# Attention outputs kept transposed, scaled in memory by GpSimd, and unit loads by eight transfers

## What is computed

```python
x = x + attention(layernorm(x), ctx, ctx)       # x, ctx: 8 x 256 x 512
x = x + ffn(layernorm(x))

# attention: 32 heads of 16, 8 key/value groups (4 heads share one)
score = einsum('bhqd,bhkd->bhqk', qh, kh) / sqrt(16)
out = einsum('bhqk,bhkd->bhqd', softmax(score), vh)
return out.transpose(0, 2, 1, 3).reshape(N, S, 512) @ Wfc.T + bfc

# ffn: router over 8 experts (2 chosen, limited by groups), gated experts of
# width 352, plus a shared gated network of width 704
return routed + (silu(h @ sg.T) * (h @ su.T)) @ sd.T
```

## Time and profile before

| what | value |
|---|---|
| median of three runs | 791.12 us |
| the profiled execution's own time | 791.93 us |
| its span, first to last instruction | 790.1 us |
| busy: TensorE, VectorE, ScalarE, GpSimd | 760.1, 579.7, 429.3, 269.3 us |
| granted TensorE clock, mean | 0.994 |
| DMA, mean over the span | 218 GB/s |

### The profile page before, as it was taken

One profiled execution on the slowest core, in us unless ns is written; L12 is line 12 of the kernel. 1 busy time (PEld: TensorE's weight loads), 2 busy tenths in 40 slices (PEclk: granted clock), 3 DMA queues, 4 the chain that ended last, 5 costly groups with the idle time before them and its releaser, 6 DMA issues.

```text
span 790.1 us, 16078 instructions
## 1 busy us (share of the span) xinstructions
PE 760.1 (96%) x5151; PEld 407.0 (52%) x5152; DVE 579.7 (73%) x1194; ACT 429.3 (54%) x843; POOL 269.3 (34%) x224
## 2 busy tenths in 40 slices
PE   6998999999999989999999999999999999999897
PEld 4553533343433325656755556555555555555553
DVE  4777779999999976998789886555555555547666
ACT  3666579999999973566433553434344343322231
POOL 3263008999993301665300101111111111015331
PEclk9999989999999999999999999999999999999999
DMA  8898846556645798998598576876777777559985
GB/s 330 324 405 245 250 139 211 185 168 194 195 121 172 228 331 295 331 376 275 173 232 225 137 173 137 187 174 175 183 175 180 179 180 173 126 164 288 288 240 150
DMA packets 161782, 172.07 MB, mean 218 GB/s; under 512 B 103680, under 2 KB 117504, under 8 KB 161216
## 3 DMA queue, kind: packets, MB, share of 16 engines
q1 hardware_dynamic: 150012, 128.89, 56.5%
q0 software_dynamic: 11120, 41.43, 16.8%
q10 hardware_dynamic: 596, 1.07, 0.4%
HBM read 105.40 MB, written 42.73 MB: 187 GB/s over the span
## 4 chain that ended last, share of the span: by engine, by line
PE 77%; DVE 10%; DMA 7%; ACT 2%; issue 2%; SPq 1%; DVEq 0%; ACTq 0%
PE psum L1467 29%; PE psum L1479 15%; PE psum L1317 8%; PE psum L1303 6%; PE psum L1231 4%; PE psum L1403 4%; PE psum L1207 4%; PE psum L1334 2%; DMA sb_weights<-in_wdn 2%; DMA sb_weights<-attn_dram 2%; PE psum L1183 1%; DMA sb_hT<-sb_h 1%; DMA sb_weights<-x_dram 1%; DMA sb_weights<-in_ctxT 1%; DVE sb_rows L1902 1%
## 5 line engine op out<-in xcount | busy, mean ns | idle before, releaser
L1467 PE MATMUL psum<-sb_weights,sb_rows 128*128 (+1 forms) x1608 | 250.8, 313 | 0.5 <-DMA sb_rows<-xnT_dram 0.5
L1467 PEld LDWEIGHTS psum<-sb_weights,sb_rows 128*128 128x128 f16 x1608 | 157.2, 98 | 91.8 <-DMA sb_rows<-xnT_dram 1.0
L1027 ACT ACTIVATE sb_weights<-psum,sb_rows 128x512 f32<-128x512 f32 x256 | 158.3, 683 | 16.9 <-PE psum L1303 15.0
L1699 DVE TENSOR_REDUCE sb_rows<-psum 128x4 f32<-128x1024 f32 x128 | 149.9, 1213 | 5.5 <-PE psum L1231 5.5
L1479 PE MATMUL psum<-sb_weights,sb_hT 128*128 (+1 forms) x630 | 147.4, 379 | 2.2 <-DMA sb_hT<-sb_h 2.2
L894 POOL DMA_INDIRECT sb_rows<-xn_rows,sb_slot_tok x39 | 38.2, 980 | 218.1 <-DVE sb_rows L2288 147.9
L1479 PEld LDWEIGHTS psum<-sb_weights,sb_hT 128*128 128x128 f16 x630 | 61.4, 98 | 67.5 <-DMA sb_hT<-sb_h 3.1
L1303 PE MATMUL psum<-sb_weights 50*128 50x512 f16 x256 | 90.0, 391 | 3.0 <-ACT sb_weights L1027 2.6
L1096 ACT ACTIVATE psum<-psum 128x352 f32<-128x352 f32 x71 | 31.8, 448 | 111.8 <-DVE psum L1949 111.8
L1317 PE MATMUL psum<-sb_weights 128*32 128x256 f32 x1024 | 82.9, 396 | 0.0
L1231 PE MATMUL psum<-sb_weights 48*128 48x256 f16 x512 | 73.2, 275 | 0.5 <-DVE sb_rows L1699 0.4
(11 more groups left out here) (264 smaller groups left out, 1017.9 us busy)
## 6 DMA issues: line engine op xcount, KB each, us to landing
sb_weights<-in_wgu SPq DMA_DIRECT2D x20, 704.0 KB, 7.4
sb_weights<-in_wgu POOLq DMA_DIRECT2D x20, 704.0 KB, 5.6
sb_weights<-in_wdn SPq DMA_DIRECT2D x17, 768.0 KB, 5.9
slot_y<-sb_rows SPq DMA_DIRECT2D x39, 256.0 KB, 2.3
sb_weights<-q_parts SPq DMA_DIRECT2D x96, 64.0 KB, 2.2
x_dram<-sb_rows SPq DMA_DIRECT2D x24, 256.0 KB, 4.6
q_parts<-sb_weights SPq DMA_DIRECT2D x16, 256.0 KB, 4.6
sb_rows<-in_x POOLq DMA_DIRECT2D x16, 256.0 KB, 4.8
```

The source lines that it names most:

```text
L1027: nc.scalar.activation(probs[G % 2][:, kt, pair * 512:(pair + 1) * 512], bank[4 + f % 2], ACT.Exp, scale=exp_scale[:, n:n + 1]).then_inc(e ...
L1467: mm = nc.tensor.matmul(bank[GU_BANKS[par][which]][:, 0:F], x_T[:, xp * D + k * P:xp * D + (k + 1) * P], gu(wp, k, which), start=(k == 0 a ...
L1699: nc.vector.tensor_reduce(to[:, :, j // UB, :, j % UB, qt], psum[:, banks[qt] * 512:(banks[qt] + 2) * 512] .rearrange("p (a h k) -> p a h ...
```

## The change

`attn_out` copies a pair of steps (both sequences of one group) in one ScalarE copy of 128x512 to `o_st`, still transposed and not yet divided. `pair_transpose`, `normalise`, `ot_transpose` and `ot_evac` are gone. SP stores each unit's output by four DMAs to `o_parts` and its sums by one to `o_sums`. Once per block SP loads the block's sums as 128x128, VectorE takes reciprocals (`sum_recs`), SP stores them to `o_recs`. GpSimd then, for each of the 16 pieces (block, quarter), loads the piece and the reciprocals, each of these repeated over 16 rows, multiplies, and stores the piece to `attnT_dram`, which the token stage loads tile by tile, four ahead, straight into the layout that `out_project` wants. Twelve pieces, two at a time, follow the loop over x; the four of the last block lie between the held weights. A unit's q and k come by eight DMAs, two of them a copy repeated over two rows. Layouts and semaphores change with it.

```diff
@@ SP
+                q_of = [q_parts[part, m, n].rearrange("(d a x) t -> a d (x t)", d=HD, a=SIDES) for part in range(2)]
+                k_of = k_parts[:, n].rearrange("s (d a x) t -> a d s (x t)", d=HD, a=KD)[m]
                 for side in range(SIDES):
...
+                    at = SIDE * side
+                    sp.dma_start(q_st[m][at:at + 2 * HD].rearrange("d g h t -> d (g h t)"),
+                                 q_of[0][side].unsqueeze(1).broadcast_to([HD, 2, HH * MG * BT])).then_inc(st_ld[m], 16)
+                    sp.dma_start(k_st[m][at:at + 2 * HD].rearrange("d g t -> d (g t)"), k_of).then_inc(st_ld[m], 16)
...
             def store_attn(u):
-                sp.wait_ge(attn_done, UG * (u + 1))
...
+                sp.wait_ge(pv_evac, MG * (u + 1))
+                n, m, st = u // KD, u % KD, o_st[u % 2]
+                sp.dma_start(o_sums[n, m].rearrange("(g c) t -> c g t", c=HPG),
+                             st[HD:HD + VW * (HPG - 1) + 1:VW]).then_inc(attn_st[u % 2], 16)
+                for c in range(HPG):
+                    sp.dma_start(o_parts[n, m].rearrange("(g c d) t -> c d g t", g=MG, c=HPG)[c],
+                                 st[VW * c:VW * c + HD]).then_inc(attn_st[u % 2], 16)
...
+            def load_sums(n):
+                for s in range(2):
+                    sp.wait_ge(attn_st[s], FREE + O_ST * KD // 2 * (n + 1))
+                sp.dma_start(sum_sb, o_sums[n].rearrange("m h (q t) -> (m h q) t", t=P)).then_inc(sum_ld, 16)
+
+            def store_recs(n):
+                sp.wait_ge(rec_done, n + 1)
+                sp.dma_start(o_recs[n].rearrange("m h (q t) -> (m h q) t", t=P), sum_sb).then_inc(rec_st, 16)
...
+                if u in (5, 9):
+                    load_sums(u // KD - 1)
+                if u in (6, 10):
+                    store_recs(u // KD - 1)
...
+            def load_attn(t):
+
+                if t >= TPB:
+                    sp.wait_ge(fc_ready, t - TPB + 1)
+                sp.wait_ge(chunk_st, 16 * KD * (t // TPB + 1))
+                sp.dma_start(oT_rows[t % TPB], attnT_dram[t].rearrange("p k t -> p (k t)")).then_inc(a_ld[t % TPB], 16)
...
                 if u == 13:
...
+                    load_sums(u // KD - 1)
                     load_ring(5)
+                    store_recs(u // KD - 1)
...
+                if u == 15:
+                    sp.wait_ge(gu_cut, CUTS_P2)
+                    for t in range(TPB):
+                        load_attn(t)
+            load_sums(BLOCKS - 1)
...
+            for t in range(TILES - 2):
+                if t + TPB < TILES:
+                    load_attn(t + TPB)
+                if t >= 2:
+                    store_lnT(t - 2, t % 2)
+                store_x2(t, t % 2)
+                if t == 3:
+                    store_recs(BLOCKS - 1)
+                load_res_rows(t // 2 + 1, t % 2)
+                store_xn2(t, t % 2)
@@ GpSimd
+            def load_chunk(i):
+                n, m, s = i // KD, i % KD, chunk_set(i)
+                pool.wait_ge(rec_st, 16 * (n + 1))
+                if i > 1:
+                    pool.wait_ge(chunk_st, 16 * (i - i % 2))
+                nc.gpsimd.dma_start(chunk_raw[s], o_parts[n, m]).then_inc(chunk_ld, 16)
+                nc.gpsimd.dma_start(chunk_rec[s],
+                                    o_recs[n, m].unsqueeze(1).broadcast_to([MG * HPG, HD, BT])).then_inc(chunk_ld, 16)
+
+            def scale_chunk(i, loaded):
+                n, m, s = i // KD, i % KD, chunk_set(i)
+                pool.wait_ge(chunk_ld, 32 * loaded)
+                nc.gpsimd.tensor_tensor(chunk_raw[s], chunk_raw[s], chunk_rec[s], ALU.mult).then_inc(chunk_done, 1)
+                pool.wait_ge(chunk_done, CHUNK_SEEN + i + 1)
+                nc.gpsimd.dma_start(attnT_dram[n * TPB:(n + 1) * TPB, :, m, :].rearrange("a p t -> p a t"),
+                                    chunk_raw[s].rearrange("p (a t) -> p a t", a=TPB)).then_inc(chunk_st, 16)
...
+            for first in range(0, 3 * KD, 2):
+                for i in range(first, first + 2):
+                    load_chunk(i)
+                for i in range(first, first + 2):
+                    scale_chunk(i, first + 2)
...
-            pool.wait_ge(attn_done, UNITS * UG)
+            pool.wait_ge(pv_evac, UNITS * MG)
             pool.wait_ge(dn_max_done, NE + SH)
             for h in range(3):
                 load_held(h)
+            last = (BLOCKS - 1) * KD
             for c in range(CUTS_P2, CUTS):
 
                 h = c - CUTS_P2
+                if h == 0:
+                    for i in range(last, last + 2):
+                        load_chunk(i)
                 if h % 2 == 0:
                     scale_weights(c)
                     second_part(c)
                 else:
                     pool.wait_ge(gu_cut_v, h // 2 + 1)
+                if h == 1:
+                    for i in range(last, last + 2):
+                        scale_chunk(i, last + 2)
+                    for i in range(last + 2, last + 4):
+                        load_chunk(i)
+                if h == 3:
+                    for i in range(last + 2, last + 4):
+                        scale_chunk(i, last + 4)
@@ ScalarE
+            def attn_out(p):
+
+                u, g = p // MG, p % MG
+                act.wait_ge(pv_ready, UB * (p + 1))
+                act.wait_ge(attn_st[u % 2], FREE + O_ST * (u // 2))
+                nc.scalar.copy(o_st[u % 2][:, g, :], bank[6]).then_inc(pv_evac, 1)
...
             def first_part(h):
 
+                if h >= 2 * (HELD - 1):
+                    act.wait_ge(chunk_st, 16 * UNITS)
@@ TensorE
+            def out_project(t, r, n):
+                pe.wait_ge(a_ld[r], n * 16 + (16 + A_SEEN))
@@ VectorE
+            def sum_recs(n):
+
+                dve.wait_ge(sum_ld, 16 * (n + 1))
+                nc.vector.reciprocal(sum_sb, sum_sb).then_inc(rec_done, 1)
...
+                if j == 1 and u % KD == 2 and u > KD:
+                    sum_recs(u // KD - 1)
```

199 lines of the change are left out of this document (57 added, 142 removed).

## The result

The changed kernel takes 877.18 us (median of four runs, 874.98 to 879.98) against 791.73 (four runs, 790.06 to 796.26) for the kernel before: 1.106 times as long, 95% interval 1.102 to 1.110. The forecast was 834, with a range of 808 to 858: the sign and the place were right, the size was about half.

What follows compares the result with a forecast made beforehand. Attention was taken as shared by three engines, token tiles as paced by TensorE. GpSimd's six serial pairs (76.6 us) and held chain end the token stage 42 us later: 790.1 + 42 = 832, named 834, range 808 to 858.

Steps and rivals of the forecast that it cites:

- The path: Token stage: held weights load only after GpSimd's six pairs, so the stage stands still and ends at 426, 42 us later.
- The start of the pairs: GpSimd after the bias loop: pairs begin at 267.3 us; slowed bias tiles could move that up to 5 us later.
- c = 12.2: GpSimd, one serial pair of pieces: four loads, two multiplies, two stores, 12.2 us; first two pairs 13.9, six pairs 76.6.
- L: GpSimd pair: time from the fourth load's issue to its landing, taken as 3.5 us; median over the whole kernel 4.8.
- The bound of 13.9: GpSimd pair: upper bound of its length in us, from both landing medians of the whole kernel; 13.9 throughout gives 846.
- S: GpSimd pair: time from the second store's issue to its landing, taken as 3.3 us.
- rival (c): GpSimd's piece stores: many short runs are slow, 3.4 us more per pair, 27 us in all, 861; chance 0.12.
- 15 less the 3 to 5 given back: Attention: pairs of steps fall to about 5.3 us, 15 us over 32 pairs; the stage then ends near 285.
- Three to five us given back: Last two attention units: VectorE's block 2 reciprocals wait for sums by an SP round trip, costing 3 to 5 us.
- (a): GpSimd's pairs stay hidden: 15 us from attention and 8 from the token tiles come off, about 770; chance 0.05.
- (b): GpSimd's pairs are quicker, 9 us each, and the held chain costs nothing more: 802; chance 0.10.
- The clock: TensorE after the token stage's stand-still: granted clock under 1 at about 350 would add some us on top.

Runs made afterwards that it cites:

- the ceiling: Changed kernel without GpSimd's scaling and without the sums' loads, reciprocals and stores (outputs unscaled): 0.997 of the kernel before; with SP's unit loads first as well, 1.002.

## Why the prediction fell short

**The path was right.** Held loads after all pairs, first held cut one landing later (5.4 us, predicted 6), GpSimd standing for block 3's reciprocals until P + 11.7 (predicted P + 12.8), tenth cut at P + 69.3 (predicted P + 65), 22 us from there to the stage's end (19.7), last stage 408 (406.1). P is the issue of the held loads. With the chain 4.3 us, the stage's end 2.3 and the last stage 2 us longer than forecast, these add some 8.6 us to the forecast's span of 832.

**The start of the pairs** was 271.8 and not 267.3: the last bias tile waited 4.5 us for its load beside the down weights. The forecast named this risk of up to 5 us and left it out of the sum.

**The step that failed is the pair, c = 12.2.** The forecast had one pair at 12.2 us (13.9 for the first two) and took its waits from transfers that were alone. Six pairs came to 107.0 us, 17.8 each, where the forecast's terms give 73.9 to the same point: 33 of the 46 us that are missing from the span. Its terms, measured:

- L, the landing of the fourth load. Taken 3.5 (4.8 in the first two pairs), together 23.6 us; measured as the waits ahead of the first multiply plus the fourth issue, 45.6 + 6 x 0.65 = 49.5: 26 us more (the landings themselves are 10.2, 10.1, 8.5, 5.4, 9.4 and 5.4, 49.0). Rows of the changed kernel for the load of the reciprocals:

```profile
  POOL sb_weights L867: 45.6, 6
...
DMA to landing us min/median/max: 4.3/6.3/10.2
```

The mistake was to take L from the earlier trace rows, where GpSimd has one load and one store under way at a time. A pair has four loads of 256 KB in flight, half of them reading their source 16 times; without SP's tile traffic, that is 4.9 + 0.65 = 5.5 us (the run with tiles held back), 9.5 us over six pairs more than assumed. The other 16 us lie in four of the pairs, with waits of 9.6, 9.5, 8.0 and, in the fifth, 8.8 us. Of these 16, 7 are shown to be SP's tile traffic, because they go when it is held back (third and fifth pair); the 9 of the first two pairs are put down to SP's down weights and stores by argument only. The bound of 13.9 was too low for the same reason: it was worked out from medians of single transfers. By the Trainium skill, "DMA: Bandwidth & Descriptors", section "Anatomy of one DMA", a load of 256 KB would have been 2.6 us, an estimate from its figures; the least rows of before, 3.0 and 2.3 us, lie on either side of it and don't meet it. No load of the pairs landed under 2.9 us, and the reciprocals' median is 6.3, so the measurement decides against that figure here.

- S, the store's landing: waits of 7.2, 2.5, 2.5, 2.5 and 2.8 us ahead of the next pair; with the issue of 0.8 each, 4 us more than taken, nearly all in the first.
- The 512 short runs, rival (c): the issue takes 0.80 to 0.84 us against 0.56 in the earlier trace rows. That is 0.5 us a pair and not 3.4. Taking nothing was nearly right, and this rival's 861, though nearest to the result, stood for the wrong reason.
- Multiplies and gaps as taken, within 0.4 us a pair, the last one aside.

**Attention gained 5 us, not 15 less the 3 to 5 given back.** The last copy starts at 288.94 against 294.15; with the scatter, 284.0 to 289.4, one execution tells this gain to no better than some 5 us. In the rows of the profiled execution two terms were mis-sized. A pair of steps is 5.52 us and not 5.3: the exponentials' own pitch of 0.58 was right, but ScalarE's short waits for TensorE's scores, which the forecast took to be gone with the transposes, remain (steps of 0.65 and 0.81 us). And a loop was missing from the sum: SP issues 15 transfers a unit as before, but the chain maxima, rows, loads, landing has less room in a shorter unit. By the forecast's 10.6 us a unit that chain had to fit into 1.1 us less than the 11.70 of before; from 142 to 215 the units took 12.1, where TensorE waits for keys and for part of the time runs at its lower clock. The forecast checked SP's number of issues and not its latency. Neither error reached the total, since the chain on GpSimd starts from its own time.

**"Three to five us given back"** for the sums was 12.2 us of VectorE standing, and about 6 us of SP's order. What of it reached the end, between nothing and 5 us, the one execution without it doesn't tell.

**Rivals.** (a) was ruled out rightly; the ceiling says more, that even its 770 could not have come, since without any scaling the kernel takes 791 to 793 us. The 23 us that it counted as gain (15 in attention, 8 in the tiles) are not there: a tile stays at over 5 us without TensorE's transposes, with VectorE the busiest engine after it (75 of 84 us, as busy as TensorE). The sum took 2 us off the stage's tail for the absent transposes, and wrongly: 22 us of it are left. (b) fell with c, which was above 12 us in every pair. (c) is dealt with above.

**The clock.** As the forecast feared, it fell with the stand-still: 0.50 in stretches of the token stage, 0.73 over it. The first output projection at 1.2 GHz:

```profile
380.72 6.58 PE L1419 MATMUL psum<-sb_weights 128*128 128x512 f32 x8 [91.43 <-DMA sb_weights<-attnT_dram]
```

That row is from the kernel with tiles held back; the earlier trace rows has 3.60 for the same work at 2.4 GHz. The clock was 0.50 in the 10 us up to 380 and 0.55 over that row. How much of the lower clock is on the path was not measured; GpSimd's chain, which sets the stage, does not depend on it where it waits for its own transfers.

## What to carry over

A serial chain on one engine with waits for its own transfers is priced by how many transfers are in flight and by what the other queues move at that time, not by the landing of a lone transfer in a quiet stretch; for a burst, the forecast's bounds should have reached at least to the longest landings in the rows (8.0 us in the earlier trace rows) and not to medians. Before counting work that is removed as time, ask in each stage for the next resource by its busy time, and for loops through an issuing queue (signal, issues, landing, use) by their latency against the new, shorter period. And look at what is queued behind such a chain: here it was the loads of the held weights, so that the chain's length moved the start of the last stage.

## What was not expected of the hardware

A 256 KB load on GpSimd's queue landed in 3.0 to 3.6 us where it was the only load there. With two in flight such loads landed in 2.9 to 7.0 us in one and the same kernel (the run with one load a piece), beside different traffic of SP. GpSimd's issue of a direct transfer was 0.80 us with 512 runs and 0.56 with 128 (stores), and 0.64 where the source is repeated against 0.54 where it is not (loads). A store of 256 KB, 2.9 us by its median landing, took 7.5 beside three loads of 768 KB, though the DMA engines' mean share over attention, in whose last microseconds it lies, was 0.64: averages over a stage hide such bursts.
